# Phase A tile by tile instead of in batches of four, and layer-norm work moved between two engines, in a transformer block with eight experts

## The chip, the cores and the metric

The kernel runs on all 8 cores of one Trainium2 chip. Each core holds half a sequence of 4096 tokens as its own 2048 tokens; there is no exchange between cores. The metric is the device time of the slowest core in microseconds.

## The reference

```python
xn = layernorm(x)                                     # x: (4, 4096, 1024) f32, no gain
# attention block on xn
Q = elu(xn @ Wq + bq) + 1;  K = elu(xn @ Wk + bk) + 1;  V = xn @ Wv + bv
KV = K^T V;  Ksum = sum_s K                           # per head, 16 heads of 64
Z = 1 / (Q . Ksum + 1e-6)
a = ((Q KV) * Z) @ Wo + bo
x1 = layernorm(xn + a) * g1 + beta1
y  = relu(x1 @ W1 + b1) @ W2 + b2                     # 1024 -> 4096 -> 1024
attn = layernorm(x1 + y) * g2 + beta2
# expert block on xn: h = mod(int(xn[:,0] + xn[:,1]), 8); experts h and h+1, weight 1/2 each
ffn = sum_e w_e * (relu(xn @ W1[e] + b1[e]) @ W2[e] + b2[e])
out = x + attn + ffn
```

## The kernel before

The program is written as five lists of instructions, one for each engine: T is TensorE (PE), V is VectorE (DVE), S is ScalarE (ACT), G is GpSimd (POOL) and Y is SyncE (SP). Within a list the order is the order of the code, and an engine works through its own list in order. Waits and increments on semaphores are written by hand: `wait(engine, semaphore, value)`, `inc`, and `chain`, which increments and makes the same engine wait until its own last instruction has finished (`vbar` is `chain` on V). There is no planner.

The stages are, with a barrier of all engines between them:

- Phase A (`emit_phase_a`, line 375): 32 tiles of 128 tokens, the core's own 16 and the other half's 16. Of each tile it makes the row statistics, normalises it, transposes it into bf16, projects it to K and V, applies elu+1 to K and adds K'V to an accumulator. Then comes a tail that makes the routing weights.
- The experts (`emit_moe`): 8 experts, all tokens of the core through each.
- B1 (`emit_b1`): Q, the attention output, the projection with Wo, and the residual sum into `x1_sb`.
- The first layer norm (`emit_ln(1)`), the feed-forward layer B2, the second layer norm (`emit_ln(2)`), and the output B4.

Phase A works on batches of four tiles. For a batch, `stats_sums` is issued for all four tiles: SP loads a tile of x into one of the four slots of `xtm_a`; DVE sums each row (L400) and scales the sum (L402); ACT squares (L407) and subtracts the mean (L409); DVE sums the squares (L412). `stats_finish` then makes the inverse deviation of the four tiles at once: Ln and Exp on ACT (L427, L429), four small steps on DVE (L432 to L438), and on ACT one scaling of each tile (L446), with three one-column copies for an own tile. Only then do the four tiles run, one after the other: `emit_trans` (transposes L503 in two waves through one PSUM bank, copies L514), `emit_proj` (K with L525 and its bias L529 in PSUM banks 0 and 1, V with L537 and L541 in banks 2 and 3), elu (DVE max L464, ACT Exp L475, DVE min and sum L485, DVE copy of V L491) and `emit_kv` (L556, L559, and three additions on DVE).

In B1, after Q, for each pair of heads PE broadcasts z into PSUM bank 5 (L885), ACT copies it to `zb` (L891), PE multiplies q with the KV matrix (L894), and DVE multiplies the two (L901). PE's next L885 waits until ACT has copied the last one. Afterwards sixteen half tiles of x are loaded one by one into the single buffer `xt_b1`, normalised (L922) and transposed (L930).

A layer norm has four passes of 512 tokens. In a pass DVE copies each of the eight feature chunks to bf16 (L983) and squares it (L984), and PE sums both over the features (L989, L991). A chain of operations on one row follows (L998 to L1020, with Ln and Exp on ACT), PE broadcasts the two rows (L1024, L1026), and DVE applies them chunk by chunk: subtract (L1033), multiply (L1035), gain and offset (L1038 or L1046), and then the bf16 copy for B2 (L1043, first norm) or the addition to the expert sum (L1051, second norm). Each of these waits for the one before it.

## Time and profile before

| | us |
|---|---|
| median of 3 runs | 6113.13 |
| lowest and highest | 6109.89, 6130.52 |
| the profiled execution | 6128.27 |
| its span on the slowest core (core 1) | 6126.7 |
| spans of the other cores | 6090.8 to 6124.7 |
| PE busy | 4876.7 (80%) |
| DVE busy | 1789.6 (29%) |
| ACT busy | 994.4 (16%) |
| phase A without its tail | 43.5 to 820 |
| first and second layer norm | 5022 to 5193, 5849 to 6029 |

The span goes from the first to the last instruction of a core; the rest of the profiled execution's time lies outside it. The times in the profile are from that one execution, so a sum made from them stands against 6128.27, not against the median. Busy shares are averages over stages that have different limits.

### The profile page before, as it was taken

To read this page: it belongs to the slowest core of one execution; us is meant where nothing else is said; L and a number is where in the kernel's file an instruction comes from. 1 tells how busy PE (TensorE), PEld (TensorE's weight loads), DVE (VectorE), ACT (ScalarE), POOL (GpSimd) and SP (SyncE) were. 2 spreads that over 40 slices of the span, in tenths; PEclk is the share of its full clock that TensorE was granted. 3 is DMA by queue.
4 is the path that set the end of the run, shared out by engine and by line. 5 is a ranking of instruction groups with operands and counts; after the bars stand their busy time and mean duration, and the time that the engine had idled before them with its cause. 6 is when DMAs were issued, how large, how long until landed. Compare 5 with 4: busy or idle time off the path is not lost.

```text
span 6126.7 us, 55582 instructions; the slowest of 8 cores (6090.8 to 6126.7 us)
## 1 busy us (share of the span) xinstructions
PE 4876.7 (80%) x21665; PEld 2132.5 (35%) x21665; DVE 1789.6 (29%) x3391; ACT 994.4 (16%) x1853; POOL 344.5 (6%) x661
## 2 busy tenths in 40 slices
PE   3445449999999999999999999999996542777732
PEld 1222214444444444444444444444432110333301
DVE  2333332222222222222222222222224236111164
ACT  2222211111111111111111111111111110111100
POOL 1000000000000000000000000000000000000000
PEclk9777679999999999999999999988998665999965
DMA  2000002222222222222222222222212110111103
GB/s 56 21 21 24 18 10 37 38 37 37 40 35 38 38 35 38 38 35 38 38 36 37 39 36 38 39 32 35 38 28 37 41 36 4 28 28 23 28 2 110
DMA packets 105680, 209.45 MB, mean 34 GB/s; under 512 B 12960, under 2 KB 13232, under 8 KB 105424
## 3 DMA queue, kind: packets, MB, share of 16 engines
q0 software_dynamic: 91056, 163.84, 17.6%
q1 hardware_dynamic: 14368, 42.06, 2.1%
q8 instruction: 177, 2.90, 0.2%
q14 instruction: 79, 0.65, 0.0%
HBM read 361.06 MB, written 8.39 MB: 60 GB/s over the span
## 4 chain that ended last, share of the span: by engine, by line
PE 75%; DVE 12%; ACT 6%; DMA 3%; issue 3%; DVEq 0%; POOL 0%; ACTq 0%; SPq 0%; POOLq 0%
PE ps L730 30%; PE ps L768 29%; PE ps L1067 4%; PE ps L1088 4%; PE ps L525 3%; DMA xt_b<-xs 1%; ACT h_b L1077 1%; PE ps L774 1%; DMA xtm_b<-xs 1%; DVE x_sb L1105 1%; DVE ln_t L1033 1%; DVE ln_t L1035 1%; PE ps L503 1%; DVE vtm L491 1%; DVE ktm L485 1%
## 5 line engine op out<-in xcount | busy, mean ns | idle before, releaser
L730 PE MATMUL ps<-xnbf,w1s 128*128 128x512 bf16 x8192 | 1842.6, 384 | 54.0 <-DVE wb L715 32.7
L730 PEld LDWEIGHTS ps<-xnbf,w1s 128*128 128x128 bf16 x8192 | 803.0, 99 | 1060.3 <-issue 153.4
L768 PE MATMUL ps<-h_hi,w2s 128*128 128x512 bf16 x4096 | 938.2, 389 | 22.5 <-DVE acc L792 22.5
L768 PE MATMUL ps<-h_lo,w2s 128*128 128x512 bf16 x4096 | 906.4, 379 | 0.0
L792 DVE TENSOR_TENSOR acc<-acc,ps 128x512 f32<-128x512 f32 x992 | 614.8, 681 | 853.2 <-PE ps L768 536.0
L768 PEld LDWEIGHTS ps<-h_hi,w2s 128*128 128x128 bf16 x4096 | 408.0, 100 | 533.0 <-issue 93.5
L768 PEld LDWEIGHTS ps<-h_lo,w2s 128*128 128x128 bf16 x4096 | 401.2, 98 | 484.4 <-issue 5.1
L740 ACT ACTIVATE h_lo<-ps,eb_sb 128x512 bf16<-128x512 f32 x512 | 310.2, 689 | 1566.5 <-PE ps L730 1566.5
L740 ACT ACTIVATE h_hi<-ps,eb_sb 128x512 bf16<-128x512 f32 x512 | 310.2, 689 | 1469.0 <-PE ps L730 1469.0
L748 DVE TENSOR_TENSOR h_lo<-h_lo,wb 128x512 bf16<-128x512 bf16 x512 | 183.1, 419 | 963.1 <-ACT h_lo L740 963.1
L748 DVE TENSOR_TENSOR h_hi<-h_hi,wb 128x512 bf16<-128x512 bf16 x512 | 183.1, 420 | 901.9 <-ACT h_hi L740 901.9
L1067 PE MATMUL ps<-c_bf,w1s 128*128 128x512 bf16 x1024 | 243.0, 398 | 102.5 <-ACT h_b L1077 75.8
L1088 PE MATMUL ps<-h_b,w2s 128*128 128x512 bf16 x1024 | 238.9, 394 | 91.2 <-DVE x_sb L1105 58.8
L503 PE MATMUL ps<-ident,xtm_a 128*128 128x128 f32 x256 | 53.0, 343 | 324.8 <-ACT xn L453 155.1
L292 POOL DMA_DIRECT2D w2s<-ew_pk x256 | 135.1, 528 | 1753.9 <-PE ps L768 1188.8
L292 POOL DMA_DIRECT2D w1s<-ew_pk x256 | 135.3, 529 | 1708.2 <-PE ps L730 1708.2
L1067 PEld LDWEIGHTS ps<-c_bf,w1s 128*128 128x128 bf16 x1024 | 102.0, 102 | 244.1 <-issue 140.1
L1105 DVE TENSOR_TENSOR x_sb<-x_sb,ps 128x512 f32<-128x512 f32 x96 | 59.5, 681 | 421.5 <-PE ps L1088 421.5
L1088 PEld LDWEIGHTS ps<-h_b,w2s 128*128 128x128 bf16 x1024 | 100.9, 101 | 229.2 <-issue 123.1
L989 PE MATMUL ps<-ln_bf,onescol_bf 128*1 128x512 bf16 x64 | 31.5, 491 | 168.4 <-DVE ln_bf L984 168.2
L1077 ACT ACTIVATE h_b<-ps,b_sb 128x512 bf16<-128x512 f32 x128 | 77.6, 689 | 525.2 <-PE ps L1067 525.2
L503 PEld LDWEIGHTS ps<-ident,xtm_a 128*128 128x128 f32 x256 | 34.3, 170 | 333.3 <-issue 333.3
(169 smaller groups left out, 2203.1 us busy)
## 6 DMA issues: line engine op xcount, KB each, us to landing
w1s<-ew_pk POOLq DMA_DIRECT2D x256, 256.0 KB, 3.5
w2s<-ew_pk POOLq DMA_DIRECT2D x256, 256.0 KB, 3.5
xtm_a<-xs SPq DMA_DIRECT2D x32, 512.0 KB, 3.3
xt_b<-xs SPq DMA_DIRECT2D x32, 256.0 KB, 2.6
w1s<-w_pk POOLq DMA_DIRECT2D x32, 256.0 KB, 3.6
w2s<-w_pk POOLq DMA_DIRECT2D x32, 256.0 KB, 3.6
xtm_b<-xs SPq DMA_DIRECT2D x16, 512.0 KB, 4.0
out<-otm_b SPq DMA_DIRECT2D x16, 512.0 KB, 2.9
```

Of the source, the lines that this page charges most:

```text
L292: self.em(e, lambda x, o=out, i=in_: x.dma_start(out=o, in_=i))
L503: self.em("T", lambda t, c=c, j=j: t.transpose(ps[4][:, j * 128:(j + 1) * 128], xt[:, c * 128:(c + 1) * 128], self.ident[:]))
L525: self.em("T", lambda t, k=k, hh=hh, lh=lhs(k, g): t.matmul(ps[hh][:], lh, self.wk_sb[:, k * D + hh * 512:k * D + (hh + 1) * 512], start=( ...
L730: self.em("T", lambda t, k=k, tt=tt, slot=slot: t.matmul(ps[tt][:], self.w1t(slot, k), self.xnbf[:, k * TOWN + tt * 512:k * TOWN + (tt + 1 ...
L740: self.em("S", lambda s, tt=tt, i=i, hreg=hreg, e=e, n=n: s.activation(hreg[:, i * TOWN + tt * 512:i * TOWN + (tt + 1) * 512], ps[tt][:], ...
L748: self.em("V", lambda v, tt=tt, i=i, hreg=hreg, e=e: v.tensor_mul(hreg[:, i * TOWN + tt * 512:i * TOWN + (tt + 1) * 512], hreg[:, i * TOWN ...
L768: self.em("T", lambda t, j=j, tt=tt, slot=slot, hreg=hreg, lp=last_plain: t.matmul(ps[4 + tt][:], self.w2t(slot, j), hreg[:, j * TOWN + tt ...
L792: self.em("V", lambda v, dst=dst, tt=tt: v.tensor_add(dst, dst, ps[4 + tt][:]))
L1067: self.em("T", lambda t, k=k, tt=tt, slot=slot: t.matmul(ps[tt][:], self.w1t(slot, k), self.c_bf[:, k * TOWN + tt * 512:k * TOWN + (tt + 1 ...
L1077: self.em("S", lambda s, tt=tt, i=i, n=n: s.activation(self.h_b2[:, i * TOWN + tt * 512:i * TOWN + (tt + 1) * 512], ps[tt][:], AF.Relu, bi ...
L1088: self.em("T", lambda t, j=j, tt=tt, slot=slot: t.matmul(ps[4 + tt][:], self.w2t(slot, j), self.h_b2[:, j * TOWN + tt * 512:j * TOWN + (tt ...
L1105: self.em("V", lambda v, x=xsl, tt=tt: v.tensor_add(x, x, ps[4 + tt][:]))
```

## The change

It has three parts.

Phase A: the batches are gone. The statistics of tile g are issued together with the elu of tile g-1, piece by piece: on DVE the sum of x(g), then the max of g-1, then the sum of squares of g, then the rest of the elu of g-1 and its accumulation; on ACT the square and the subtraction of g, the Exp of g-1, then Ln and Exp of g. The small steps of the inverse deviation are made on ACT for one tile at a time. On PE the K'V of g-1 stands before the transposes of g. x has two slots instead of four.

B1: `zb` has two slots, one for even and one for odd pairs. As it now overlaps `xt_b1`, SP waits for the last product before the first load of x of each half.

Layer norms: the bf16 copy and the square are made by ACT, and so is the copy for B2. The three steps of the apply are issued staggered over neighbouring chunks, with two slots of `ln_t`.

```diff
-        self.xtm_a = sb("xtm_a", [128, 4 * D], F32, TR, 196608)
+        self.xtm_a = sb("xtm_a", [128, 2 * D], F32, TR, 196608)
...
-        self.zb = sb("zb", [128, 512], BF16, ST + 5120, 204800)
+        self.zb = sb("zb", [128, 2 * 512], BF16, ST + 5120, 204800)
...
+        def emit_stats(g, mid_v=None, mid_s=None):
...
+            if g >= 2:
+                self.wait("Y", self.s_mm, evT[g - 2])
+            evDMA[g] = self.dma("Y", xt, self.xs[g * 128:(g + 1) * 128, :], self.s_lx[par])
+            mc = self.mstat[:, g:g + 1] if own else self.scol[:, 0:1]
+            rc = self.rstat[:, g:g + 1] if own else self.scol[:, 1:2]
+            ac = self.scol[:, 2:3]
+            sq = self.elu_a[:, par * D:(par + 1) * D]
+            self.wait("V", self.s_lx[par], evDMA[g])
+            self.em("V", lambda v, xt=xt, mc=mc: v.reduce_sum(mc, xt, axis=AXX))
+            self.vbar()
+            self.em("V", lambda v, mc=mc: v.tensor_scalar_mul(mc, mc, -INV_D))
...
+            self.em("S", lambda s, xt=xt, sq=sq, mc=mc: s.activation(sq, xt, AF.Square, bias=mc))
             self.chain("S", self.s_sc)
+            self.em("S", lambda s, xt=xt, mc=mc: s.add(xt, xt, mc))
             s_sub = self.inc("S", self.s_sc, 1)
+            if mid_v is not None:
+                mid_v()
             self.wait("V", self.s_sc, s_sub)
+            self.em("V", lambda v, sq=sq, ac=ac: v.reduce_sum(ac, sq, axis=AXX))
+            self.vbar()
+            self.em("V", lambda v, ac=ac: v.tensor_scalar(ac, ac, INV_D, EPS_LN, op0=OP.mult, op1=OP.add))
+            v_ac = self.inc("V", self.s_ve, 1)
+            if mid_s is not None:
+                mid_s()
+            r0 = self.scol[:, 3:4]
+            self.wait("S", self.s_ve, v_ac)
+            self.em("S", lambda s, ac=ac, r0=r0: s.activation(r0, ac, AF.Ln))
+            self.chain("S", self.s_sc)
+            self.em("S", lambda s, r0=r0: s.activation(r0, r0, AF.Exp, scale=-0.5))
+            self.chain("S", self.s_sc)
+            self.em("S", lambda s, rc=rc, r0=r0: s.mul(rc, r0, r0))
+            self.chain("S", self.s_sc)
...
+            self.em("S", lambda s, rc=rc, r0=r0: s.mul(rc, rc, r0))
+            self.chain("S", self.s_sc)
+            self.em("S", lambda s, xt=xt, rc=rc: s.mul(xt, xt, rc))
...
+        pend = []
+        for g in range(NGL):
+            if pend:
+                pg, ek, ev = pend.pop(0)
+                emit_stats(g, mid_v=lambda pg=pg, ek=ek: elu_vmax(pg, ek),
+                           mid_s=lambda pg=pg, ek=ek, ev=ev: (elu_sexp(pg, ek),
+                                                             elu_vtail(pg, ev)))
+                emit_kv(pg)
+            else:
+                emit_stats(g)
+            ek, ev = emit_T(g)
+            pend.append((g, ek, ev))
...
-                    self.wait("S", self.s_ve, evAOZ[(p - 1) % 2] if p > 0 else evAOZ_last)
-                    self.em("S", lambda x: x.copy(self.zb[:], ps[5][:]))
+                    self.wait("S", self.s_ve, evAOZ[p % 2] if p > 1 else evAOZ_last)
+                    self.em("S", lambda x, zsl=zsl: x.copy(zsl, ps[5][:]))
...
             self.wait("T", self.s_sc, evZB)
+            self.wait("Y", self.s_ve, aoz_done)
...
-                self.wait("V", self.s_mm, evMMpar[sl])
-                self.em("V", lambda v, b1=b1, x=xsl: v.tensor_copy(b1, x))
-                self.em("V", lambda v, b2=b2, x=xsl: v.tensor_mul(b2, x, x))
-                vb = self.inc("V", self.s_ve, 1)
-                self.wait("T", self.s_ve, vb)
+                self.wait("S", self.s_mm, evMMpar[sl])
+                self.em("S", lambda s, b1=b1, x=xsl: s.copy(b1, x))
+                self.chain("S", self.s_sc)
+                self.em("S", lambda s, b2=b2, x=xsl: s.activation(b2, x, AF.Square))
+                vb = self.inc("S", self.s_sc, 1)
+                self.wait("T", self.s_sc, vb)
...
+                stages.append(("fin", c - 2))
+                stages.append(("mul", c - 1))
+                stages.append(("sub", c))
...
+                if step == "sub":
+                    prev = (tt, c - 2) if c >= 2 else (tt - 1, KC - 2 + c)
+                    self.wait("V", self.s_ve, evApply.get(prev, 0))
+                    self.em("V", lambda v, x=xsl, lts=lts: v.tensor_sub(lts, x, ps[2][:]))
+                    self.inc("V", self.s_ve, 1)
+                elif step == "mul":
+                    self.wait("V", self.s_ve, self.s_ve.n)
+                    self.em("V", lambda v, lts=lts: v.tensor_mul(lts, lts, ps[3][:]))
+                    self.inc("V", self.s_ve, 1)
...
+                    self.wait("V", self.s_ve, self.s_ve.n)
...
+                        vx = self.inc("V", self.s_ve, 1)
...
+                        self.wait("S", self.s_ve, vx)
+                        self.em("S", lambda s, csl=csl, x=xsl: s.copy(csl, x))
+                        self.chain("S", self.s_sc)
```

## Rows read from the trace of the kernel before

**Rows 1.** The page: shares by engine of the chain that ended last.

```profile
PE 75%; DVE 12%; ACT 6%; DMA 3%; issue 3%; DVEq 0%; POOL 0%; ACTq 0%; SPq 0%; POOLq 0%
```

**Rows 2.** Windows, phase A: length, busy times PE, PEld, DVE, ACT, POOL, clock, DMA.

```profile
43.50:820.00 776.50, 397.33 (x1920) 171.74 (x1920) 257.78 (x441) 207.68 (x481) 0.00 (x0) 0.75 0.06 19
```

**Rows 3.** The page's groups, phase A's transposes: busy, mean ns, idle before.

```profile
L503 PE MATMUL ps<-ident,xtm_a 128*128 128x128 f32 x256 | 53.0, 343 | 324.8 <-ACT xn L453 155.1
```

**Rows 4.** Timeline of PE, K projections: start, duration, instructions.

```profile
78.69 5.60 PE L525 MATMUL ps<-wk_sb,xnbf 128*128 128x512 bf16 x16 [1.01 <-ACT xnbf L514]
...
177.02 5.93 PE L525 MATMUL ps<-wk_sb,xnbf 128*128 128x512 bf16 x16 [1.22 <-ACT xnbf L514]
...
194.09 5.92 PE L525 MATMUL ps<-wk_sb,xnbf 128*128 128x512 bf16 x16 [1.22 <-ACT xnbf L514]
...
309.17 3.61 PE L525 MATMUL ps<-wk_sb,xnbf 128*128 128x512 bf16 x16 [1.22 <-ACT xnbf L514]
...
804.46 6.23 PE L525 MATMUL ps<-wk_sb,xnp 128*128 128x512 bf16 x16 [1.28 <-ACT xnp L514]
```

**Rows 5.** Timeline of one tile, from its V projection to the next transposes.

```profile
200.48 3.63 PE L537 MATMUL ps<-wv_sb,xnbf 128*128 128x512 bf16 x16
200.72 1.29 DVE L464 TENSOR_SCALAR elu_a<-ps 128x512 f32<-128x512 f32 x2 [8.83 <-PE ps L529]
...
207.01 0.64 PE L503 MATMUL ps<-ident,xtm_a 128*128 128x128 f32 x4
```

**Rows 6.** Timeline of the first batch's statistics.

```profile
46.56 1.22 DVE L412 TENSOR_REDUCE tpack<-elu_a 128x1 f32<-128x1024 f32 x1 [3.87 <-ACT xtm_a L409]
...
67.22 1.15 ACT L446 ACTIVATE xtm_a<-xtm_a,scol 128x1024 f32<-128x1024 f32 x1 [1.17 <-DVE scol L438]
68.45 0.19 ACT L449 COPY rstat<-scol 128x1 f32<-128x1 f32 x1
```

**Rows 7.** Groups of ACT's instructions: busy, mean ns, idle before.

```profile
L1008 ACT ACTIVATE ln_s<-ln_s 1x512 f32<-1x512 f32 x8 | 5.0, 630 | 396.0 <-DVE ln_s L1004 396.0
...
L660 ACT ACTIVATE wrow_f<-wscr,mkc_sb 8x2048 f32<-8x2048 f32 x1 | 2.0, 2002 | 0.1
...
L658 ACT ACTIVATE wscr<-h 8x2048 f32<-8x2048 f32 x1 | 1.9, 1910 | 44.3 <-DVE h L654 44.3
...
L407 ACT ACT_TABLE_LOAD x1 | 1.3, 1283 | 42.8 <-DVE scol L402 42.8
```

**Rows 8.** Timeline of B1: the loads of x, and the loop over head pairs.

```profile
4777.00 0.55 DVE L922 TENSOR_SCALAR xt_b<-xt_b,mstat,rstat 128x512 f32<-128x512 f32 x1 [3.85 <-DMA xt_b<-xs]
...
4883.32 0.58 PE L885 MATMUL ps<-zbfb,e_sb 16*128 16x512 bf16 x1 [4.50 <-DVE zbfb L879]
...
4884.05 0.59 ACT L891 CAST zb<-ps 128x512 bf16<-128x512 f32 x1 [38.66 <-PE ps L885]
...
4884.78 0.58 PE L885 MATMUL ps<-zbfb,e_sb 16*128 16x512 bf16 x1 [0.34 <-ACT zb L891]
```

**Rows 9.** Timeline of DVE, first pass of the first layer norm.

```profile
5022.01 0.43 DVE L983 CAST ln_bf<-x_sb 128x512 bf16<-128x512 f32 x1
...
5031.11 0.68 DVE L998 TENSOR_SCALAR ln_m<-ps 1x512 f32<-1x512 f32 x1 [0.85 <-PE ps L991]
...
5042.34 0.69 DVE L1033 TENSOR_TENSOR ln_t<-x_sb,ps 128x512 f32<-128x512 f32 x1 [4.07 <-PE ps L1026]
...
5064.28 0.42 DVE L983 CAST ln_bf<-x_sb 128x512 bf16<-128x512 f32 x1
```

**Rows 10.** Timeline of DVE, first pass of the second layer norm.

```profile
5848.78 0.43 DVE L983 CAST ln_bf<-x_sb 128x512 bf16<-128x512 f32 x1
...
5870.01 0.69 DVE L1033 TENSOR_TENSOR ln_t<-x_sb,ps 128x512 f32<-128x512 f32 x1 [4.07 <-PE ps L1026]
...
5894.09 0.42 DVE L983 CAST ln_bf<-x_sb 128x512 bf16<-128x512 f32 x1
```

**Rows 11.** The page's DMA issues: KB each, median us to landing.

```profile
xtm_a<-xs SPq DMA_DIRECT2D x32, 512.0 KB, 3.3
```

More of the change, by code:

```diff
@@ L498, in emit_trans, with emit_T @@
+            evA[g] = self.inc("S", self.s_sc, 1)
+        def emit_T(g):
+            nonlocal evXNw
+            own = g < NGOWN
+            par = g % 2
+            xt = self.xtm_a[:, par * D:(par + 1) * D]
             self.wait("T", self.s_sc, evA[g])
             for wave in range(2):
-                self.wait("T", self.s_sc, evXNw[0])
+                self.wait("T", self.s_sc, evXNw)
                 for j in range(4):
                     c = wave * 4 + j
-                    self.em("T", lambda t, c=c, j=j: t.transpose(
+                    self.em("T", lambda t, xt=xt, c=c, j=j: t.transpose(
@@ L509, in emit_trans @@
                 self.wait("S", self.s_mm, mmv)
-                if (g >= NGOWN) and g >= 2:
+                if (not own) and g >= 2:
                     self.wait("S", self.s_mm, evKVmm.get(g - 2, 0))
@@ L544, in emit_proj, with elu_vmax @@
                     start=False, stop=True))
-            evVmm[g] = self.inc("T", self.s_mm, 1)
+            evVmm = self.inc("T", self.s_mm, 1)
+            return evKmm, evVmm
+        def elu_vmax(g, evKmm):
+            par = g % 2
+            rt = self.elu_a[:, par * D:(par + 1) * D]
+            self.wait("V", self.s_mm, evKmm)
+            if g >= 2:
+                self.wait("V", self.s_mm, evKVmm.get(g - 2, 0))
+            for hh in range(2):
+                self.em("V", lambda v, hh=hh, rt=rt: v.tensor_scalar(
+                    rt[:, hh * 512:(hh + 1) * 512], ps[hh][:], 0.0, None, op0=OP.max))
+            evK_v[g] = self.inc("V", self.s_ve, 1)
@@ new lines, in elu_sexp @@
+        def elu_sexp(g, evKmm):
+            par = g % 2
+            kslot = self.ktm[:, par * D:(par + 1) * D]
+            self.wait("S", self.s_mm, evKmm)
+            self.wait("S", self.s_ve, evK_v[g])
+            if g >= 2:
+                self.wait("S", self.s_mm, evKVmm.get(g - 2, 0))
+            for hh in range(2):
+                self.em("S", lambda s, hh=hh, kslot=kslot: s.activation(
+                    kslot[:, hh * 512:(hh + 1) * 512], ps[hh][:], AF.Exp))
+            evK_s[g] = self.inc("S", self.s_sc, 1)
@@ new lines, in elu_vtail @@
+        def elu_vtail(g, evVmm):
+            par = g % 2
+            kslot = self.ktm[:, par * D:(par + 1) * D]
+            vslot = self.vtm[:, par * D:(par + 1) * D]
+            rt = self.elu_a[:, par * D:(par + 1) * D]
+            self.wait("V", self.s_sc, evK_s[g])
+            for hh in range(2):
+                self.em("V", lambda v, hh=hh, kslot=kslot, rt=rt: v.scalar_tensor_tensor(
+                    kslot[:, hh * 512:(hh + 1) * 512], kslot[:, hh * 512:(hh + 1) * 512],
+                    1.0, rt[:, hh * 512:(hh + 1) * 512], op0=OP.min, op1=OP.add))
+            self.vbar()
+            self.wait("V", self.s_mm, evVmm)
+            for hh in range(2):
+                self.em("V", lambda v, hh=hh, vslot=vslot: v.tensor_copy(
+                    vslot[:, hh * 512:(hh + 1) * 512], ps[2 + hh][:]))
+            evV_v[g] = self.inc("V", self.s_ve, 1)
@@ L547, in emit_kv @@
         def emit_kv(g):
-            kslot = self.ktm[:, (g % 2) * D:(g % 2 + 1) * D]
-            vslot = self.vtm[:, (g % 2) * D:(g % 2 + 1) * D]
+            par = g % 2
+            kslot = self.ktm[:, par * D:(par + 1) * D]
+            vslot = self.vtm[:, par * D:(par + 1) * D]
             self.wait("T", self.s_ve, evV_v[g])
@@ L862, in emit_b1 @@
         for s in range(2):
+            if s == 1:
+                self.wait("S", self.s_mm, max(xf_prev))
             for sub in range(2):
```

215 lines of the change are left out of this document (65 added, 150 removed).

## The prediction

> **What bounds the kernel now.** I read the chain that ended last first: TensorE (PE) holds 75% of it [rows 1], but most of that is the expert layers, which the change leaves alone. So the question is how the time of four other stages is made. I took windows by stage, then the timeline of a few tiles in each. Phase A lasts from 43.5 to 820 us with PE busy for only 397 of 776 us, at a mean granted clock of 0.75 [rows 2]. The group of PE's transposes shows where the rest went: 325 us of idle time stood before them, mostly behind ScalarE's (ACT's) last operations of the row statistics [rows 3]. They run in batches of four tiles, with nothing on PE in the meantime. Within a batch a tile takes one path with no overlap: projections, elu, K'V, transposes. The projection starts give the rates. From the first (78.69) to the last (804.46) are 725.8 us and 31 intervals [rows 4]. The 24 inside batches sum to 390.1 us, 16.25 each, the slowest 17.07 (177.02 to 194.09). The 7 across batches take the other 335.7 us, 47.96 each: 31.7 more than a tile needs.
>
> **The change, part by part.**
>
> *Phase A, gain.* Statistics of tile g are now issued between the pieces of tile g-1's elu. VectorE (DVE) sums x(g) and ACT squares and subtracts it while PE runs the K projection of g-1 (some 6.4 us in the slow tiles), against some 4 us of work, so this part is hidden. The 7 batch stalls go: 7 x 31.7 = 222 us. The first tile starts after one tile's statistics instead of four. Its second sum starts at 46.56 and lasts 1.22 [rows 6]; with the small step after it, 0.27, and two semaphores, ACT gets it at 48.15. ACT then does seven small chained operations, 2.46 us (below), the 1.15 us scaling and two copies, and transposes start near 52.4. Transposes to projection take 4.15 us there at the low clock, so the first projection starts near 56.6 and not 78.7: 22 us more.
>
> *Phase A, cost.* What is not hidden is the part behind the K projection. In order of time from the start of the V projection (200.48) [rows 5]: DVE's two max operations at 0.24, ending 1.53; behind them on DVE now the second sum, 1.22 [rows 6], and a 0.17 step, so ACT may begin at 3.1. Its chain: a small operation is 0.19 and the next starts 0.08 after it (67.22 + 1.15 = 68.37, next at 68.45) [rows 6]. A per-partition pointer operand adds 0.09: 2.002 against 1.910 us for the same shape [rows 7]. So Ln and Exp are 0.30 each, the five arithmetic steps 0.37 each, 2.46 in all; the scaling 1.15; evA comes at 6.8, and at 7.4 for one of the core's own tiles, which has two more copies. The other path, elu tail, vtm copies and K'V, now lets the transposes start at 207.01, that is 6.53 [rows 5]; the second sum ahead of it makes it some 0.13 later, 6.66. So an own tile costs 0.85 more and a foreign one 0.27 more: 15 x 0.85 + 16 x 0.27 = 17 us. Net gain of phase A: 222 + 22 - 17 = 227 us. PE waits in order for K'V and then for evA; nothing else is queued behind it.
>
> *The clock.* At the lower level, 1.2 GHz, 16 K matmuls take 5.9 us; at 2.4 GHz, 3.61 (the one at 309.17) [rows 4]. Six of the 32 K projections ran at the higher level throughout, and the V projections all did. PE's pause between two projections stays what it is inside a batch or grows by 0.3 to 0.85, so I keep the 16.25 mix. With no fast K projection an interval is about 16.6: 11 us less gained. With three of four fast, some 36 us more.
>
> *x buffers, 4 to 2.* The load of x(g) is issued when the transposes of g-2 are done, and DVE wants it some 14 us later; it lands in 3.3 us [rows 11]. Hidden. It could land up to 22 us after its issue before the chain above moved.
>
> *Phase B1.* The second zb buffer lifts DVE's hold on ACT's copy. But PE may broadcast z for the next pair only when ACT has emptied the one PSUM bank. The first pair of a group, for which DVE holds nothing up, shows that loop: PE at 4883.32, ACT's copy at 4884.05 for 0.59, PE again at 4884.78 [rows 8]: 0.73 + 0.59 + 0.14 = 1.46. The loop through DVE is 1.47 now (0.59 copy, 0.69 product, two semaphores). Both loops have the same length, so I take 1 us of gain (0 to 2). The new wait of SyncE for the last product forbids the early load of x that was in time twice; each is now exposed like the one before 4777.00, where DVE stood for 3.85 us, some 1.2 of them until PE had freed the tile [rows 8]. That is 2.6; other loads left DVE standing up to 4.46. I take 2 x 2.9 = 5.8 us lost, bounds 4 and 8.
>
> *Layer norms, statistics.* Copy and square go from DVE to ACT, where they are chained. A pass of DVE (8 columns) is 9.1 us up to the row operations [rows 9]. ACT's 512 elements from SBUF take 0.63 [rows 7]; two of them, a chain of 0.09 and an overlap of 0.10 into the next give 1.25 a column, 10 us, plus 1.0 for the last matmuls: 11.0. If they don't overlap it is 11.8. So 1.9 us are lost wherever they are exposed. The Trainium skill, ScalarE: Activation LUTs, section "Rules for kernel authors", says add, mul and relu belong on VectorE, which is up to about three times as fast there in bf16, and it speaks against this move. By its cost line (186 ns + 0.833 ns an element: an estimate of 0.61 us) the pass would be 10.8 us, 0.2 less than by the row; the trace agrees that ACT is slower. What the rule leaves out is that in the second norm ACT's work stands beside DVE's.
>
> *First norm.* The apply of a pass is 21.9 us now (5042.34 to 5064.28) [rows 9]. The c_bf cast leaves DVE: 8 x (0.43 + 0.10) = 4.2. The subtraction no longer waits for its neighbour, 0.60 instead of 0.79 (two operations of 0.69 in 1.29 [rows 5]), seven times: 1.3. It becomes 16.4. The next pass's statistics stand behind the last cast on ACT, 0.8. A pass: 11.0 + 11.2 + 16.4 + 0.8 = 39.4 against 42.3: 4 x 2.9 = 12 us gained (8 to 16).
>
> *Second norm.* Here ACT has no cast, and x1 is only read. After Ln and Exp of pass tt it can do the statistics of tt+1 during DVE's apply (24.1 us, 5870.01 to 5894.09 [rows 10]), so three of four disappear. Apply becomes 22.7 by the same 0.19. Four passes now: 4 x 45.3 = 181 (5848.78 to 5894.09). Then: 11.0 + 4 x (11.2 + 22.7) = 146.6. Gain 34 us (27 to 37).
>
> *Sum.* -227 - 1 + 5.8 - 12 - 34 = -268 us. The profiled execution took 6128.3 us (span 6126.7), 15.1 above the median 6113.1. 6128.3 - 268 = 5860, on the median's footing 5845 us.
>
> **Rivals.**
>
> *Clock better:* at least three of four K projections at 2.4 GHz, since no 28 us pauses are left: 5809. For it: fast ones come now and then [rows 4]. Against: pauses inside a batch don't shrink.
>
> *Clock worse:* V projections fall to 1.2 GHz too. Then the 18 matmuls of a V projection last 7.7 us instead of 4.1, and K's 7.7 instead of 6.5: 31 x (3.6 + 1.2) = 149 us, 5994. Against: all 32 V projections had the high level.
>
> *The second norm does not overlap* (ACT stands behind something I missed), or ACT is slower beside DVE: the three hidden passes come back, 3 x 11: 5878.
>
> *Table switches:* every Ln and Exp between Square and Copy could need a table load of 1.28 us, two a tile: 82 us, 5927. Against: one load in the whole trace, although both functions stand between squares already [rows 7]. The Trainium skill, same page, section "Table sets: the hidden batching unit", names a set that holds both; this is its rule that a switch costs time.
>
> *Slower:* with two x buffers the load becomes the bound. It moves the path from 22 us after its issue and eats the whole 268 us at 22 + 268/31 = 31 us. At 33 us the kernel would be at 5845 + 11 x 31 = 6186. Against: 3.3 us to landing, nothing else on the DMA queues in this phase.
>
> *Nothing comes of it:* in-order DVE serialises the tiles, the whole 9.9 us of a tile's statistics added to 16.25. That gives 56.6 + 31 x 26.15 = 867 us for the last projection against 804: 63 lost, 41 gained later, 6135. It needs the sum of x(g) to wait for K'V(g-1); in the order of issue it stands before it.
>
> **How the numbers follow.** Forecast 0.72; better clock 0.08; worse clock 0.05; second norm 0.07; tables 0.02; load 0.02; serialised 0.02; something smaller that I don't see 0.02. The range: the low end adds to the better clock some of the bounds of the norms, 5795; the high end takes the missed overlap and the slow clock mix, 5890. It leaves out the lower clock, tables and the last rivals. A median of this kernel can be told from no change at 0.3%, 18 us; every case but the last two is beyond that. So faster 0.95, same 0.02, slower 0.03.
>
> **What would show it.** Phase A's projection starts are 16 to 17.5 us apart without 48 us steps, and the last is near 577. The transposes start 6.8 to 7.4 after the V projection. The z loop stays at 1.47. There is one table load. DVE's first row operation in the first norm comes 11 us after the start, and in the second norm right behind the last apply. Wrong would be: intervals above 18 us, waits of DVE for x, a V projection of 7 us, ACT idle during the second norm's apply.

## The result and the profile after

| | before | after |
|---|---|---|
| median, 10 runs each | 6132.09 us | 5914.63 us |
| lowest | 6109.44 us | 5857.50 us |
| forecast | | 5845 us (5795 to 5890) |

The ratio is 0.9611, 95% interval 0.9572 to 0.9651. The forecast was 5845 / 6113.13 = 0.9562. So it is faster, by 3.9% instead of 4.4%, and the median lies above the range. In four of the ten executions after and two of the ten before, and in the profiled one of the changed kernel, the cores of one die have a lower granted clock and take longer, so the ratio compares the other six (5857.50 to 5916.93 us, mean 5888.0) with the other eight (mean 6126.1), and the rows of the changed kernel below are of die 1. The view by core, with span and mean granted clock:

```profile
core 2: 6122.3 us, clock 0.856
...
core 6: 5839.6 us, clock 0.908
```

I take core 6 of both profiles, which had an undisturbed clock each time. The numbered rows of the kernel before are of core 1, its slowest; in phase A the two cores hardly differ (first and last K projection at 78.69 and 804.46 us on core 1, 78.38 and 804.79 on core 6). The first matmul of each stage gives its length. The view by source line, changed kernel, core 6: duration in ns (least, median, most), first and last start; the lines are the experts' hidden layer, Q, the first matmul of B2 and the transposes of B4:

```profile
L726 PE MATMUL ps<-xnbf,w1s x8192: 376/379/634, 669.4 to 4278.2; 128*128 128x512 bf16 x200
...
L823 PE MATMUL ps<-xnbf,w1s x256: 376/379/635, 4397.9 to 4475.9; 128*128 128x512 bf16 x128
...
L1090 PE MATMUL ps<-c_bf,w1s x1024: 376/379/635, 4945.8 to 5506.7; 128*128 128x512 bf16 x171
...
L1146 PE MATMUL ps<-ident,acc x128: 418/421/448, 5739.8 to 5826.4; 128*128 128x128 f32 x128
```

| stage, core 6 | before | after | change | forecast |
|---|---|---|---|---|
| start to the experts' first matmul | 885.3 | 669.4 | -215.9 | -227 |
| experts | 3730.3 | 3728.5 | -1.8 | 0 |
| B1, to the first norm's first operation | 372.4 | 381.9 | +9.5 | +4.8 |
| first norm, to B2's first matmul | 177.6 | 166.0 | -11.6 | -12 |
| B2 and second norm, to B4's first transpose | 826.3 | 794.0 | -32.3 | -34 |
| output | 99.3 | 99.8 | +0.5 | 0 |
| span | 6091.2 | 5839.6 | -251.6 | -268 |

**Phase A.** The group of the transposes and a window, changed kernel, core 6, against [rows 2, 3]:

```profile
L455 PE MATMUL ps<-ident,xtm_a 128*128 128x128 f32 x256 | 58.5, 371 | 99.5 <-ACT xn L441 61.4
```

```profile
40.00:595.00 555.00, 401.45 (x1884) 175.26 (x1884) 241.56 (x405) 257.42 (x671) 0.00 (x0) 0.80 0.09 29
```

The idle time before the transposes fell from 325 to 99.5 us. The clock column needs care: 0.80 against 0.75 looks like a gain, but the 0.75 takes in the batch stalls. Two windows inside batches of the kernel before, core 1 (the eight of them have 0.81 to 0.86), and then the changed kernel from its first to its last K projection, core 6:

```profile
78.70:128.40 49.70, 37.73 (x180) 16.00 (x181) 15.68 (x27) 7.90 (x30) 0.00 (x0) 0.86 0.10 33
...
469.20:518.40 49.20, 36.95 (x181) 16.17 (x182) 15.68 (x27) 7.90 (x30) 0.00 (x0) 0.81 0.10 32
```

```profile
54.00:590.00 536.00, 394.07 (x1862) 171.90 (x1861) 238.86 (x401) 248.66 (x650) 0.00 (x0) 0.79 0.09 30
```

So while tiles run, the granted clock is lower than before. PE's K projections, changed kernel, core 6, against [rows 4]:

```profile
53.80 5.51 PE L475 MATMUL ps<-wk_sb,xnbf 128*128 128x512 bf16 x16 [1.01 <-ACT xnbf L466]
...
123.45 6.51 PE L475 MATMUL ps<-wk_sb,xnbf 128*128 128x512 bf16 x16 [1.22 <-ACT xnbf L466]
...
402.01 5.48 PE L475 MATMUL ps<-wk_sb,xnp 128*128 128x512 bf16 x16 [1.41 <-ACT xnp L466]
...
589.56 5.57 PE L475 MATMUL ps<-wk_sb,xnp 128*128 128x512 bf16 x16 [1.31 <-ACT xnp L466]
```

The 48 us steps are gone. The first projection starts at 53.8 and the last at 589.56, which is 31 intervals of 17.28 us. An interval of the forecast was 16.8. Not one of the 32 K projections is fast throughout; on cores 1 and 6 of the kernel before, six were. Yet the mean of all 32 is the same, 5.45 us on core 1 before and on core 6 after (5.53 and 5.54 on cores 5 and 7). The reason lies in their matmuls. A K projection that is not fast begins at the lower level and rises on the way: of the 16 matmuls of the one at 177.02 [rows 4], the first eleven last 0.58 or 0.63 us each, the last four 0.38. Before, 26 of 32 projections begin so, with 11.2 matmuls at the lower level on average; after, all 32 do, but with 9.1. What did get slower are PE's transposes. The second wave of a tile, core 1 of the kernel before and core 6 of the changed one:

```profile
785.63 0.86 PE L503 MATMUL ps<-ident,xtm_a 128*128 128x128 f32 x4 [1.06 <-ACT xnp L514]
```

```profile
399.51 1.09 PE L455 MATMUL ps<-ident,xtm_a 128*128 128x128 f32 x4 [1.06 <-ACT xnp L466]
```

Before, it lasts 0.63 to 1.09 us (0.85 on average inside the batches), after it always lasts 1.09. The path of one foreign tile (one of the other half's 16) from its V projection, changed kernel, core 6, against [rows 5]:

```profile
390.88 3.63 PE L487 MATMUL ps<-wv_sb,xnp 128*128 128x512 bf16 x16
391.12 1.29 DVE L505 TENSOR_SCALAR elu_a<-ps 128x512 f32<-128x512 f32 x2 [7.65 <-PE ps L479]
392.33 1.21 DVE L414 TENSOR_REDUCE scol<-elu_a 128x1 f32<-128x1024 f32 x1
...
393.89 0.20 ACT L422 ACTIVATE scol<-scol 128x1 f32<-128x1 f32 x1 [0.24 <-DVE scol L416]
...
396.42 1.15 ACT L436 ACTIVATE xtm_a<-xtm_a,scol 128x1024 f32<-128x1024 f32 x1
...
397.82 0.63 PE L455 MATMUL ps<-ident,xtm_a 128*128 128x128 f32 x4 [0.27 <-ACT xtm_a L436]
```

ACT gets the sum 3.01 us after the V projection's start (forecast 3.1), its seven small operations take 2.53 (2.46), and the transposes start at 6.94 (6.8). For an own tile they start at 7.5 (7.4).

**B1.** The loop over pairs and the load of x behind it, changed kernel, core 6, against [rows 8]:

```profile
4519.99 0.58 PE L885 MATMUL ps<-zbfb,e_sb 16*128 16x512 bf16 x1 [0.34 <-ACT zb L891]
...
4520.72 0.58 ACT L891 CAST zb<-ps 128x512 bf16<-128x512 f32 x1 [0.87 <-DVE q_sb L902]
4521.40 0.69 DVE L902 TENSOR_TENSOR q_sb<-ps,zb 128x512 bf16<-128x512 f32 x1 [0.76 <-ACT zb L891]
4522.18 9.84 SPq L292 DMA_DIRECT2D xt_b<-xs  x3
4525.06 0.55 DVE L924 TENSOR_SCALAR xt_b<-xt_b,mstat,rstat 128x512 f32<-128x512 f32 x1 [2.96 <-DMA xt_b<-xs]
```

The loop takes 1.45 us (4518.54 to 4519.99), as before. SP issues the load only behind the last product, and DVE stands 2.96 us for it.

**The norms.** First pass of the second norm, changed kernel, core 6: the statistics' first operation, the row operation behind them, ACT's next statistics, the apply, and the next pass's row operation, against [rows 10]:

```profile
5591.60 0.62 ACT L986 CAST ln_bf<-x_sb 128x512 bf16<-128x512 f32 x1 [81.81 <-DVE dum L298]
...
5603.19 0.68 DVE L1002 TENSOR_SCALAR ln_m<-ps 1x512 f32<-1x512 f32 x1 [11.69 <-PE ps L995]
...
5607.38 0.60 ACT L986 CAST ln_bf<-x_sb 128x512 bf16<-128x512 f32 x1
...
5614.69 0.69 DVE L1050 TENSOR_TENSOR ln_t<-x_sb,ps 128x512 f32<-128x512 f32 x1 [4.00 <-PE ps L1029]
...
5636.82 0.69 DVE L1074 TENSOR_TENSOR acc<-acc,ln_t 128x512 f32<-128x512 f32 x1
5637.43 0.67 DVE L1002 TENSOR_SCALAR ln_m<-ps 1x512 f32<-1x512 f32 x1
```

The row operation of pass two stands directly behind the last apply, so the statistics are hidden: a pass is 34.2 us instead of 45.3. There is one table load in the whole trace, as before:

```profile
L407 ACT ACT_TABLE_LOAD x1 | 1.3, 1283 | 39.9 <-DVE mstat L402 39.9
```

### The profile page after: what moved, and what is told of

Read it like the earlier page. It is cut to its first block, busy times and chain, and to the rows that moved or that the text cites. A ratio compares the mean times of both kernels' runs of the same rounds, so it can differ in the third digit from the quotient of the medians.

```text
span 6122.3 us, 55579 instructions; the slowest of 8 cores (5839.6 to 6122.3 us)
## 1 busy us (share of the span) xinstructions
PE 5119.9 (84%) x21246; PEld 2200.9 (36%) x21665; DVE 1698.2 (28%) x3207; ACT 1139.5 (19%) x2205; POOL 344.4 (6%) x661
## 4 chain that ended last, share of the span: by engine, by line
PE 80%; DVE 8%; ACT 4%; DMA 4%; issue 3%; POOL 0%; DVEq 0%; SPq 0%; ACTq 0%; POOLq 0%
PE ps L726 31%; PE ps L764 31%; PE ps L1090 4%; PE ps L1111 4%; PE ps L475 3%; PE ps L487 2%; DMA xt_b<-xs 1%; ACT h_b L1100 1%; DMA xtm_b<-xs 1%; PE ps L770 1%; PE ps L455 1%; DVE x_sb L1128 1%; DVE ln_t L1050 1%; DVE vtm L534 1%; PE ps L953 1%
## 5 line engine op out<-in xcount | busy, mean ns | idle before, releaser
L726 PE MATMUL ps<-xnbf,w1s 128*128 128x512 bf16 x8027 | 1947.0, 401 | 65.4 <-DVE wb L711 32.4
L726 PEld LDWEIGHTS ps<-xnbf,w1s 128*128 128x128 bf16 x8192 | 830.7, 102 | 1148.9 <-issue 516.4
L764 PE MATMUL ps<-h_hi,w2s 128*128 128x512 bf16 x4008 | 970.3, 400 | 28.5 <-DVE acc L788 22.9
L764 PE MATMUL ps<-h_lo,w2s 128*128 128x512 bf16 x4015 | 959.4, 397 | 5.2
L764 PEld LDWEIGHTS ps<-h_lo,w2s 128*128 128x128 bf16 x4096 | 414.6, 101 | 529.2 <-issue 196.9
L932 PE MATMUL ps<-ident,xt_b 128*128 128x128 f32 x128 | 34.8, 427 | 119.3 <-DVE xt_b L924 119.3
L505 DVE TENSOR_SCALAR elu_a<-ps 128x512 f32<-128x512 f32 x64 | 41.2, 685 | 263.0 <-PE ps L479 263.0
```

What stands on the lines that cost most here:

```text
L726: self.em("T", lambda t, k=k, tt=tt, slot=slot: t.matmul(ps[tt][:], self.w1t(slot, k), self.xnbf[:, k * TOWN + tt * 512:k * TOWN + (tt + 1 ...
L764: self.em("T", lambda t, j=j, tt=tt, slot=slot, hreg=hreg, lp=last_plain: t.matmul(ps[4 + tt][:], self.w2t(slot, j), hreg[:, j * TOWN + tt ...
```

## The experiments

The tables give the length of a stage as the range over the 8 cores of the run's profile, made as in the table above. "Phase A" is the time to the experts' first matmul; the second norm goes from B2's last addition (`x_sb<-x_sb,ps`) to B4's first transpose. For comparison, all cores of before, and the four undisturbed ones of after:

| kernel | phase A | experts | B1 | first norm | second norm |
|---|---|---|---|---|---|
| before | 885 to 895 | 3729 to 3765 | 371.8 to 373.8 | 175.6 to 178.0 | 180.1 to 181.2 |
| after, cores 4 to 7 | 669 to 675 | 3728 to 3730 | 380.0 to 381.9 | 165.7 to 166.5 | 149.0 to 149.1 |

### Phase A alone

```diff
 # kernel before, with:
-    emit_phase_a (batches of four)      -xtm_a [128, 4 * D]
+    emit_phase_a (tile by tile)         +xtm_a [128, 2 * D]
```

> The kernel before with the new phase A alone (its code and its buffers); layer norms and phase B1 are those of before. My theory: phase A pays nearly all of the change. On like cores the step from start to the experts' first matmul fell by 216 us between the two kernels (885.3 to 669.4), so this run should be 216 us under the kernel before (ratio 0.965), with the same 53.8 us to the first K projection, intervals of 17.5 (own tiles) and 17.0 (foreign ones), and no K projection at the higher clock level throughout. Rival, that part of the missing 11 us of phase A comes from the neighbourhood (another state of the clock left by something else in the changed kernel): then the first K projection or the intervals differ from those of the changed kernel by more than 0.2 us and the gain is 227.

Measured: ratio 0.9643, interval 0.9624 to 0.9662, best 5890.03 us. Phase A lasts 670 to 674 us. Its intervals are 17.6 us for own and 17.2 for foreign tiles, and no K projection is fast. Theory confirmed: the loss against the forecast is made inside phase A. The run also shows how B1's own time scatters with its old code, 372.7 to 378.0.

### The norms alone

```diff
 # kernel before, with:
-    emit_ln (statistics and c_bf cast on V)
+    emit_ln (statistics and c_bf cast on S, apply in stages)
```

> The kernel before with the new layer norms alone. My theory: the norms' gains are their own, 11.5 us in the first and 32 in the second, 44 in all: ratio 0.993, the first norm 166 us long and the second 148. Rival, that the second norm's gain needs the rest of the change: 178 us instead of 148 and a ratio of 0.998.

Measured: 6062.01 and 6064.52 us against 6109.27, 45 to 47 us less, with no interval (four runs). First norm 165.3 to 166.8, second 148.7. Theory confirmed.

### B1 as it was

```diff
-    self.wait("Y", self.s_ve, aoz_done)
-    zsl = self.zb[:, (p % 2) * 512:(p % 2 + 1) * 512]
+    # ACT copies every pair into the one zb, behind product p - 1
```

> The changed kernel with phase B1 as it was before (one z buffer, no wait of SyncE for the last product). One look: read from the trace, on an undisturbed die. My theory: the 9 us by which B1 grew (372.5 to 381.9 on core 6) are the new wait of SyncE and the loads of x behind it, so B1 returns to 372 to 374 and the first load of each group is there when DVE wants it. Rival: the 9 us are the spread of the 32 loads of x, each of which DVE waits for, and B1 stays at 377 to 382. A second rival, that the second z buffer itself costs something, would show in the z loop, now 1.46 us, going to less than 1.44.

Measured: B1 373.4 to 376.2 us, against 380.0 to 381.9. So the edit in B1 costs some 7 us. The other kernels with the old B1 have 371.3 to 378.0 and five more with the new one 377.2 to 382.6, so it is the edit and not the scatter, though single cores touch. The last product of a group and the first normalisation of x, this run, core 6:

```profile
4526.91 0.69 DVE L897 TENSOR_TENSOR q_sb<-ps,zb 128x512 bf16<-128x512 f32 x1 [0.78 <-ACT zb L887]
4527.52 0.54 DVE L918 TENSOR_SCALAR xt_b<-xt_b,mstat,rstat 128x512 f32<-128x512 f32 x1
```

They start 0.61 us apart; in the changed kernel it was 3.66 (4521.40 to 4525.06). Twice 3.05 is 6.1 of the 7 us, and the loop over pairs takes 1.46 us here too. The run takes back the wait and the second z buffer together, but the loop, in which the buffer works, did not change and the loads behind the wait did. So the first theory holds: SyncE's wait costs it, not the second z buffer.

### Phase A with PE's pauses filled

```diff
+    for _ in range(6):                       # behind the V projection
+        t.matmul(ps[4][:], wk_sb[:, 0:128], wk_sb[:, 0:512], start=True, stop=True)
+    for _ in range(3 + wave):                # behind each wave of transposes
+        t.matmul(ps[0][:], wk_sb[:, 0:128], wk_sb[:, 0:512], start=True, stop=True)
```

> The changed kernel with 13 more matmuls of 512 columns a tile in phase A, which compute nothing that is used, put where PE stands: 6 after the V projection (into the bank of the transposes, before K'V), 3 and 4 behind the two waves of transposes (into the bank of K). They last 0.2 us each at the higher clock level and 0.4 at the lower. Theory: in the changed kernel K projections run at 1.2 GHz because PE pauses between V projection and K projection. With the pauses filled the second wave of transposes goes from 1.09 to 0.63 us and a K projection from 5.45 to 3.61: 2.3 us a tile, 72 us in all, under the changed kernel (ratio to before near 0.950). Rival: the clock follows the load of the whole chip or PE's mean work and not the pauses, so more matmuls leave K at 5.4 or slower, and the fillers at 0.43 us overrun their gaps by some 0.5 us a tile: 15 us or more above the changed kernel (ratio 0.962 to 0.965).

Measured: 5779.96 us, ratio 0.9473, interval 0.9442 to 0.9503: faster than the changed kernel, with 13 more matmuls a tile. Window and timeline of PE on core 6:

```profile
40.00:560.00 520.00, 420.04 (x2288) 187.85 (x2330) 261.06 (x498) 258.73 (x673) 0.00 (x0) 0.97 0.10 31
```

```profile
396.16 0.63 PE L455 MATMUL ps<-ident,xtm_a 128*128 128x128 f32 x4 [0.28 <-ACT xtm_a L436]
396.63 0.81 PE L465 MATMUL ps<-wk_sb 128*128 128x512 bf16 x3
397.86 0.63 PE L455 MATMUL ps<-ident,xtm_a 128*128 128x128 f32 x4 [0.42 <-ACT xnp L473]
398.53 0.81 PE L465 MATMUL ps<-wk_sb 128*128 128x512 bf16 x3
399.76 3.61 PE L482 MATMUL ps<-wk_sb,xnp 128*128 128x512 bf16 x16 [0.41 <-ACT xnp L473]
```

The granted clock is 0.97 instead of 0.80, which is the 2.4 GHz level nearly all the time. From the second on, all K projections take 3.61 us, and the second wave of transposes takes 0.63. The last K projection starts at 517.27 instead of 589.56: 72.3 us, the 72 of the theory. Of the 2.34 us by which an interval falls, 1.71 lie between the starts of K and V projection, 0.56 in the transposes and 0.07 in the path from the V projection to them. Shown: the K projections and the transposes are slow because of what PE does before them. The run does not tell a shorter pause from more work on PE, as the fillers are both. The Trainium skill, TensorE: Matmul & The Clock Gate, section "HAM oscillation — how this bites in real kernels", describes a kernel that falls back to the low clock in every step because PE waits in each; the trace agrees, as all 32 K projections of the changed kernel begin at the lower level.

### ScalarE's chain shortened

```diff
-    Exp -> r0;  rc = r0*r0;  rc *= ac;  rc *= -0.5;  rc += 1.5;  rc *= r0   # S, chained
+    Exp -> rc
     s.mul(xt, xt, rc)
+    evA[g] = self.inc("S", self.s_sc, 1)     # before the two own copies
```

> The changed kernel with ScalarE's chain of phase A cut: the five small arithmetic steps between Exp and the scaling (the refinement of the reciprocal root) are left out of the computation, 1.95 us, and the two own copies stand behind the event that lets the transposes start. Theory (my prediction's): two paths lead from the V projection to the transposes, ScalarE's chain (now 6.9 us, 7.5 for own tiles) and K'V (6.6). So the cut gives only the difference: 0.3 us for a foreign tile (17.0 to 16.7), 0.9 for an own one (17.5 to 16.6), 19 us in all, last K projection near 570 on core 6 instead of 589.6, and no K projection faster. Rival: the chain alone is the bound, then a tile falls by 1.95 and the last K projection comes near 527.

Measured: the last K projection starts at 552.76, 36.8 us earlier, and the phase lasts 630 to 635. Neither theory had it. An own tile on core 6, fast K projection and what leads to it:

```profile
121.60 3.63 PE L479 MATMUL ps<-wv_sb,xnbf 128*128 128x512 bf16 x16
...
128.13 0.64 PE L447 MATMUL ps<-ident,xtm_a 128*128 128x128 f32 x4
...
131.84 3.40 PE L467 MATMUL ps<-wk_sb,xnbf 128*128 128x512 bf16 x15 [1.44 <-ACT xnbf L458]
```

(One of the 16 matmuls has no record here.) The two paths are as I had them: with the chain cut the transposes start 6.53 us after the V projection, the same as in the kernel before [rows 5], and K'V is then the bound. But eight of the 32 K projections are fast again, and the mean interval is (552.76 - 51.15) / 31 = 16.18 us. On core 6 of the kernel before it was 16.09 inside a batch. Of the 1.10 us by which the interval falls, 0.69 lie between V projection and transposes (mean 7.25 to 6.56) and 0.4 in the transposes and K projections. So the 0.4 to 1.0 us by which the change lengthens the path is paid twice, once as path and once through the clock: of the 34 us of 31 intervals, some 21 and 13.

### Statistics two tiles ahead

```diff
-    for g: stats(g) around elu(g-1); K'V(g-1); transposes(g); K(g), V(g)
+    for g: K(g); statistics 1 of g+2; wave 0 of g+1; elu(g); V(g);
+           statistics 2 of g+2; wave 1 of g+1; copy of V(g); K'V(g); load(g+4)
```

> The changed kernel with another order in phase A: the statistics run two tiles ahead (four x buffers again), the first wave of transposes of tile g+1 stands behind K projection g and the second behind V projection g, K'V(g) last; the small arithmetic is on VectorE. Nothing that PE does waits for statistics then. Theory: PE's pauses are what costs phase A, twice: as idle time and through the clock. Both K and V projection take 3.6 us, and VectorE (9 us of work a tile, with the wait for ScalarE's square in it) sets a tile near 12 us: last K projection near 430 on core 6, 150 to 160 us under the changed kernel (ratio to before 0.932 to 0.936). Rival: the clock does not stay up (K projections of 5 us), or VectorE's in-order queue delays the copies of V: 14.5 us a tile, 85 us under the changed kernel (0.945).

Measured: 5739.59 us, ratio 0.9391, interval 0.9350 to 0.9431. Phase A lasts 556 to 558 us, 115 less than in the changed kernel; an interval is 13.7 us, between the theory (12) and the rival (14.5). DVE sets it, core 6:

```profile
390.04 1.22 DVE L422 TENSOR_REDUCE tpack<-elu_a 128x1 f32<-128x1024 f32 x1 [1.34 <-ACT elu_a L417]
...
394.39 1.29 DVE L539 SCALAR_TENSOR_TENSOR ktm<-ktm,elu_a 128x512 bf16<-128x512 bf16 x2 [1.41 <-ACT ktm L533]
```

It stands 1.34 us for ACT's square and 1.41 for its exponential in each tile. On six cores 15 of the 32 K projections are fast, on cores 2 and 5 only four, and their interval is the same (13.75 us), so PE's clock hardly sets the tile any more.

### Two banks for z

```diff
-    self.wait("T", self.s_sc, evZB)
-    ps[5]                                    # broadcast of every pair
+    self.wait("T", self.s_sc, evZBp[p % 2])
+    ps[5 - p % 2]                            # broadcasts in turns
```

> The changed kernel with two PSUM banks for the broadcast of z in B1 (the second z buffer is in it already). Theory (my prediction's): the second z buffer gave nothing because the one bank makes the same loop of 1.46 us (PE, ScalarE's copy, PE). With two banks VectorE's product of 0.69 us sets the rate, 0.75 to 0.85 us a pair: 32 pairs, some 20 us less, B1 near 361 instead of 381. Rival: PE's order (the product of Q and M waits for the product before last, and the next broadcast stands behind it) sets it: 1.1 us a pair, 11 us less. Second rival, that buffers are not the bound at all: no change.

Measured: B1 366.9 to 374.2 us, some 10 us less. The loop on core 6:

```profile
4493.86 0.60 PE L886 MATMUL ps<-zbfb,e_sb 16*128 16x512 bf16 x1
...
4494.40 0.61 PE L896 MATMUL ps<-q_sb,m_sb 128*128 128x512 bf16 x1
...
4494.94 0.60 PE L886 MATMUL ps<-zbfb,e_sb 16*128 16x512 bf16 x1
```

The bank was the bound, as the prediction said: 1.45 goes to 1.08 us. The rate is the rival's (1.1), but not by its wait; what comes next is a third thing. Two matmuls start 0.54 us apart with no wait between them: PE itself, at a granted clock of 0.50 there, makes the pair.

### Two x buffers in B1

```diff
-    self.wait("Y", self.s_ve, aoz_done)      # before the first load
-    self.wait("Y", self.s_mm, max(xf_prev))  # one buffer
+    zsl = self.zb[:] if p % 2 == 0 else self.elu_r[:]
+    xt = self.xt_b1[:] if fh == 0 else self.xt_b1b[:]   # over zbfb and zb
+    self.wait("Y", self.s_mm, xf_prev[fh])
```

> The changed kernel with the buffers of B1 placed otherwise: the second z buffer takes the place of the elu scratch, which is free by then, so SyncE need not wait for the last product before it loads x; and the place of z and of the reciprocals serves as a second x buffer for every other half tile. Theory: B1 loses 7.5 us by SyncE's wait (381 against 373.5 on seven other cores and kernels), and a half tile takes 4.87 us because each load is issued only when the transposes of the one before are done. With two in flight a half tile takes 2.4 to 2.6: B1 near 300. Rival: two loads share one queue and each takes longer, 3.5 us a half tile: B1 near 330. Third: only the wait is gone, 374.

Measured: B1 304.7 to 308.7 us, 75 less. DVE's normalisations on core 6:

```profile
4542.95 0.55 DVE L925 TENSOR_SCALAR xt_b1b<-xt_b1b,mstat,rstat 128x512 f32<-128x512 f32 x1 [2.45 <-DMA xt_b1b<-xs]
...
4547.84 0.55 DVE L925 TENSOR_SCALAR xt_b1b<-xt_b1b,mstat,rstat 128x512 f32<-128x512 f32 x1 [2.77 <-DMA xt_b1b<-xs]
```

Two half tiles in 4.89 us where one took 4.84 (4529.83 to 4534.67 in the changed kernel). That is the theory's rate, and two loads in flight do not slow each other: a load lands after 2.7 or 2.8 us (median), as before with 2.7. Some 7 of the 75 us are SyncE's wait, by the run with the old B1.

### Statistics between the casts

```diff
     s.copy(csl, x)                           # cast of pass tt, chunk c
+    if tt < 3:
+        stat_col(tt + 1, c)                  # copy and square of pass tt + 1
```

> The changed kernel with the layer norms' statistics of pass tt+1 issued column by column between ScalarE's casts of pass tt, instead of behind them. Theory: in the first norm the statistics (11 us a pass) stay exposed only because the casts to c_bf stand in front of them in ScalarE's queue; casts and statistics together are 8 x 1.85 = 14.8 us, less than VectorE's apply of 16.4, so three of the four passes' statistics disappear: the first norm 166 to 133 or 136 us, the second stays at 149. Rival: beside VectorE's reads of the same PSUM and SBUF ScalarE is slower, or a cast now waits behind a square and delays the second one: 145 to 155. Third: PE's in-order wait holds the row matmuls: no change.

Measured: first norm 139.7 to 140.7 us, second 149.0. The gain is 26 of the 30 to 33 us of the theory. The row operation of the second pass, core 6:

```profile
4829.34 0.68 DVE L1007 TENSOR_SCALAR ln_m<-ps 1x512 f32<-1x512 f32 x1 [4.00 <-PE ps L996]
```

DVE stands 4.0 us there, because ACT's last column runs only behind the last cast. The order was the bound, but its end stays exposed.

### One tile further ahead

```diff
+    s1_sum(g + 3)      # DVE, while ACT makes the exponential
+    s1_sq(g + 3)       # ACT, at the end of step g
     s1_red(g + 2)      # DVE, its square is a step old
```

> As the run with statistics two tiles ahead, and the sum of x and the square one tile further ahead still. There a tile took 13.2 us, with VectorE standing 1.34 us for ScalarE's square and 1.41 for the exponential in each. Theory: VectorE's queue sets the tile, so with the two sums moved into these pauses a tile falls by some 1.3 to 1.5 us, to 11.8, and K projections, every other one of which ran at the lower level, get fast: experts start near 515 instead of 557. Rival: PE sets it, through its copies of V (wait of 1.6 us before K'V) and the clock: 12.8 us, 545.

Measured: phase A ends at 523 to 525 us on six cores, at 541 and 543 on the other two; the window from 54 to 500 us has a granted clock of 0.87 on core 6 and 0.80 on core 4. The theory's gain came (33 of 42 us), its clock did not: on core 6, 11 of the 32 K projections are fast. The same program differs by 18 us between cores. Cores 4 and 5, the late ones, have fewer fast K projections (six and three), but that is not all: PE's matmuls themselves are slower there, in the V projections too. The matmuls of V for own tiles, window from 60 to 445 us, core 4 and then core 6:

```profile
L523 PE MATMUL ps<-wv_sb,xnbf x256: 379/435/438, 60.7 to 269.4; 128*128 128x512 bf16 x128
```

```profile
L523 PE MATMUL ps<-wv_sb,xnbf x256: 379/379/379, 61.0 to 255.7; 128*128 128x512 bf16 x128
```

On core 5 a V projection takes 4.10 us on average against 3.62 on core 6, and a K projection 4.90 against 4.65.

### All together

```diff
 # changed kernel, with the edits of the last five experiments, in one
```

> All that helped in one kernel: the deeper order of phase A, two banks for z, two x buffers in B1 without SyncE's wait, overlapped statistics in both norms. The gains lie in different stages, so they should add: against the changed kernel 160 us in phase A (115 if the deeper order gives nothing more), 75 + 10 in B1, 31 in the first norm: 276 us, 5575 us, ratio to before 0.912. Rival: the denser program lowers the granted clock in the stages behind (experts longer than 3730 us): above 0.92.

Measured: 5598.14 us, lowest 5595.30, ratio 0.9145, interval 0.9097 to 0.9192. That is 262 us under the changed kernel's lowest, not 276: phase A gave 146 of its 160. One of the seven executions took 22242.68 us, and nothing here explains it; the profile below is of another one.

> The same kernel as the last one, for a profile of an ordinary execution. If the gains add, each stage lasts what it lasted alone: experts' first matmul at 524 us, experts 3730, B1 381 - 75 (x buffers, 306) - 10 (z banks) = 296, first norm 140, second 149; 5596 us in all. If the stages act on each other, one of them is off by more than 3 us; the clock in the experts is the rival's place.

Measured on the 8 cores: phase A 522 to 524, experts 3729 to 3733, B1 292.4 to 298.8, first norm 140.5 to 142.2, second 148.6. The gains add to within 3 us in every stage but B1, where the cores scatter from 292.4 to 298.8 around the 296 expected. The view by source line, core 6, of the experts and of Q:

```profile
L766 PE MATMUL ps<-xnbf,w1s x8027: 376/379/634, 523.7 to 4133.9; 128*128 128x512 bf16 x196
...
L863 PE MATMUL ps<-xnbf,w1s x251: 376/379/631, 4256.0 to 4334.1; 128*128 128x512 bf16 x126
```

## Why the prediction was right and where it failed

**Right.** The mechanism of each part. The batch stalls went and nothing took their place. The first tile came earlier than forecast (53.8 against 56.6, 2.8 us). The DVE and ACT chain of a tile came out within 0.14 us, the loop over z within 0.01, one table load, both norms within 2 us, and the loads of x in phase A were hidden: no 48 us step and no wait of DVE for x stands in that phase's rows. None of the six rivals came: V projections at 3.63 us exclude the worse clock, and the missing fast K projections the better one.

**The step that failed in phase A: "The clock".** It said "PE's pause between two projections stays what it is inside a batch or grows by 0.3 to 0.85, so I keep the 16.25 mix". The second half does not follow from the first. Last minus first K projection was forecast at 577 - 56.6 = 520.4 us and measured at 535.8, 15.4 more. The mean interval, put together from the starts on PE:

| us, mean | before, core 1, inside batches | after, core 6 |
|---|---|---|
| K projection to V projection | 5.92 | 5.92 |
| V projection to transposes | 6.56 | 7.25 |
| first to second wave of transposes | 1.67 | 1.77 |
| second wave to next K projection | 2.10 | 2.34 |
| interval | 16.25 | 17.28 |

The second line was forecast to grow by 0.55 and grew by 0.69, which is 4 us over 31 intervals. The third and fourth were put at no change and grew by 0.34, some 11 us; that is the time of the transposes, which now run at the lower level more often. The prediction's own alternative, "no fast K projection", also says 11 us, and no K projection is fast, but the agreement is luck: the K projections cost nothing more on average. (Against core 6 before, where an interval inside batches was 16.09 us, they cost 0.18.) The slip starts in the reading that 16 K matmuls take 5.9 us at the lower level: the projections of 5.9 us are a mix, with the last matmuls at the higher level, and 16 that start 0.43 us apart would take some 7.0, an estimate from the eleven at the start of the one at 177.02. Two runs show that the clock is the cause: with the path back at 6.53 us some fast projections come back (eight of 32, mean interval 16.18), and with the pauses filled all but the first are fast and the transposes too. I had treated the mix as a constant of the kernel; it moves with what PE does in the pauses.

**B1, mis-sized.** The term for the loads was 5.8 us and the whole edit 4.8; it measured some 7 (B1 381 against 373.5 to 374.5). The bounds, 4 and 8, held it. That the second z buffer gives nothing while one bank remains is shown.

**Norms.** The row of 0.63 for ACT was right (0.60 to 0.63), but a column is 1.24 or 1.34 us instead of 1.25, so a pass's statistics are 11.6 us instead of 11.0. The Trainium skill, ScalarE: Activation LUTs, section "Rules for kernel authors", wants additions and products on VectorE, not ScalarE, which speaks against the move. For the copy the trace agrees, 0.60 to 0.62 us on ACT against 0.43 on DVE [rows 9]. For the square it does not: 0.63 on ACT against 0.68 on DVE. The kernel before, core 1:

```profile
L984 DVE TENSOR_TENSOR ln_bf<-x_sb x64: 680/683/685, 5022.3 to 5991.9; 128x512 bf16<-128x512 f32 x64
```

On DVE the square starts 0.34 us after the copy; on ACT, behind `chain`, it starts 0.7 us after it. So a column that was 0.94 us (the first four of a pass) is 1.24 or 1.34. In the second norm the time of an idle engine still paid 32 us, and in the first the same came out of it once the order was right (26 us more).

**The sum, and the step that took the median out of the range.** Stage by stage 251.6 us came, 16 less than 268: 11 in phase A, 5 in B1, 2 in the norms, against 2 that the experts gave. That alone would have been inside the range: 6113.1 - 251.6 = 5861.5 us. The median of ten is 53 us above this (the median before rose by 19 us from three runs to ten). What my sum put at nothing is a lower granted clock on some cores. The profile before showed it in small size, 3764.5 us for the experts on its slowest core against 3730.3 on core 6, and I left it out without a reason. In the profile after, the experts took 3978.4 us on core 2 (mean clock 0.856) against 3728.5 on core 6 (0.908). The two executions in the middle of the ten, 5912.33 and 5916.93 us, have mean clocks of 0.897 and 0.895 on their slowest cores, while a core at 0.906 or more takes 5839 to 5856 us in every one. The same holds for the ratio, which puts the gain at 238 us (0.0389 x 6113.1) and not at 251.6. Why the clock falls there, and whether the change makes it more frequent, is not settled.

**Open.** Which K projections come at the higher level when PE's pauses are shorter but not gone. On core 6 of the runs it was none, six, eight, 11, 15 or all but the first of 32, and no rule for it is shown.

## What to carry to other kernels

When a change makes PE's path between two blocks of matmuls even half a microsecond longer, price the matmuls and transposes behind it at both clock levels, one by one, as a block can begin at one level and end at the other; do not carry over the mix of the kernel before. Filling a wait with matmuls that compute nothing is a quick test of what the clock costs, and real work moved into the wait (here, transposes and statistics of later tiles) is the better filling. A second buffer pays only where no other single resource closes the same loop, so follow the loop through the PSUM bank and the engine's own rate before adding one.

## What was not expected of the hardware

Thirteen useless matmuls a tile made the kernel 79 us faster than the changed one's lowest run (5778.2 against 5857.5). On core 6, 72 of them are there at the last K projection, nearly all through the granted clock (0.97 against 0.80). Two cores of the same program in the same execution differ by 18 us in phase A through it (clock 0.80 and 0.87, a 512-column matmul of V 435 and 379 ns). And the same kernel can lose its fast projections without its K projections getting longer on average: 5.45 us with six of 32 fast and with none.
